# Two fp32 product stages in eight array tiles each, a third stage's four banks, and two products of the main stage in another place

## The reference, cut to what matters

```python
W = W_sess[session_ids]                        # [64 batches, 32, 64]
h = einsum('bct,bch->bht', x * cmask, W) + b   # 64 hidden values, per batch
h = gelu(h)                                    # erf form
out = einsum('bht,hs->bst', h, W2) + b2        # back to 32
c = out * tmask
x = x + (c.astype(fp16) @ W16 + bias)          # W16: int4 weights unpacked, 512 x 512
```

## Time and profile before

| | |
|---|---|
| median of 3 runs | 200.32 us (200.03 to 200.41) |
| the profiled execution | 200.16 us, of it a span of 198.4 us from first to last instruction |
| granted TensorE clock | 1.0 of full speed over the span |
| TensorE busy | 187.1 us (94%) |
| VectorE busy | 131.1 us (66%) |
| ScalarE busy | 69.2 us (35%) |
| GpSimd busy | 62.9 us (32%) |

### The profile page before, as it was taken

The page is one execution under the profiler, slowest core; times in us unless marked ns, Lnnn a source line. Parts: engine busy times, 40 slices in busy tenths (PEclk is TensorE's granted clock), DMA queues, the critical chain, the costliest instruction groups (busy, mean ns, idle before and its releaser), DMA issues.

```text
span 198.4 us, 3202 instructions
## 1 busy us (share of the span) xinstructions
PE 187.1 (94%) x962; PEld 124.1 (63%) x962; DVE 131.1 (66%) x319; ACT 69.2 (35%) x134; POOL 62.9 (32%) x91
## 2 busy tenths in 40 slices
PE   2889999789999999999999999999999999999993
PEld 1778656456675556565656566565667678688882
DVE  3697995477733677878785867577662689522961
ACT  0557636224314435552545344543522300031000
POOL 5273200000552266425652453321347223111000
PEclk9999999999999999999999999999999999999999
DMA  4899506069696252225112521151244943633993
GB/s 142 272 309 217 183 4 208 0 194 327 150 386 232 73 160 76 60 60 163 53 55 60 165 63 53 53 159 43 80 134 137 348 153 113 198 114 106 362 344 143
DMA packets 25785, 30.50 MB, mean 154 GB/s; under 512 B 7464, under 2 KB 16808, under 8 KB 25768
## 3 DMA queue, kind: packets, MB, share of 16 engines
q1 hardware_dynamic: 21968, 20.25, 32.5%
q0 software_dynamic: 3328, 9.96, 16.2%
q10 hardware_dynamic: 472, 0.09, 0.2%
HBM read 19.54 MB, written 6.55 MB: 132 GB/s over the span
## 4 chain that ended last, share of the span: by engine, by line
PE 90%; DVE 3%; DMA 2%; issue 2%; ACT 1%; SPq 0%; DVEq 0%
PE ps L1103 19%; PE ps L1015 9%; PE ps L1051 8%; PE ps L1027 8%; PE ps L988 6%; PE ps L962 6%; PE ps L1078 4%; PE ps L1061 4%; PE ps L1107 3%; PE ps L1076 3%; PE ps_ct L1103 3%; PE ps L1090 3%; PE ps L1003 2%; DMA x_all<-in_L_ffn_W 2%; PE ps_ct L1039 2%
## 5 line engine op out<-in xcount | busy, mean ns | idle before, releaser
L1103 PE MATMUL ps<-G,xT_all 128*128 128x512 f32 x168 | 48.9, 414 | 0.0
L341 POOL DMA_INDIRECT lz<-L_z_dram,idx_l x16 | 16.1, 1009 | 80.5 <-PE ps L1090 52.0
L1103 PEld LDWEIGHTS ps<-G,xT_all 128*128 128x128 f32 x168 | 29.0, 189 | 15.2 <-issue 11.0
L392 ACT ACTIVATE xT_all<-ps 128x512 fp32r<-128x512 f32 (+1 forms) x36 | 14.8, 453 | 43.8 <-PE ps L1061 33.9
L548 DVE TENSOR_TENSOR xT_all<-ps,xT_all 128x512 fp32r<-128x512 f32 (+2 forms) x37 | 18.9, 512 | 16.2 <-ACT xT_all L392 15.7
L448 ACT ACTIVATE gel<-ps,bsess 128x512 f32<-128x512 f32 x32 | 20.3, 684 | 17.2 <-PE ps L1015 17.2
L350 POOL DMA_INDIRECT WT<-L_dram,idx_l x16 | 15.3, 958 | 21.3 <-PE ps L1107 16.5
L324 POOL DMA_INDIRECT wsel<-in_L_cond_W_sess,idx_w x16 | 17.3, 1084 | 7.2 <-DVE onehot L552 4.2
L548 DVE TENSOR_TENSOR x_all<-x_all,ps 128x512 f32<-128x512 f32 x21 | 13.5, 682 | 8.8 <-PE ps L1239 8.6
L1015 PE MATMUL ps<-x_all,wbd 64*128 64x512 f32 x64 | 18.1, 641 | 0.0
L1051 PE MATMUL ps<-W,cT 128*128 128x512 f16 x64 | 16.6, 382 | 1.3 <-issue 1.2
(11 more groups left out here) (188 smaller groups left out, 274.5 us busy)
## 6 DMA issues: line engine op xcount, KB each, us to landing
az<-AT SPq DMA_DIRECT2D x64, 64.0 KB, 1.8
out<-x_all SPq DMA_DIRECT2D x15, 256.0 KB, 2.8
x_all<-in_x SPq DMA_DIRECT2D x3, 1024.0 KB, 6.4
L_dram<-xT_all SPq DMA_DIRECT2D x4, 512.0 KB, 8.9
x_all<-in_L_ffn_W SPq DMA_DIRECT2D x2, 512.0 KB, 4.3
x_all<-in_L_cond_base_weight SPq DMA_DIRECT2D x4, 256.0 KB, 7.4
x_all<-in_x SPq DMA_DIRECT2D x2, 512.0 KB, 5.9
x_all<-in_L_cond_lora_B_w SPq DMA_DIRECT2D x4, 256.0 KB, 8.0
```

What stands on the lines that cost most here:

```text
L341: nc.gpsimd.indirect_dma_start(lz[:, t % 2, :].bitcast(F32), None, L_z_dram, bass.IndirectOffsetOnAxis(idx_l[:, t:t + 1], 0)).then_inc(s_l ...
L392: return nc.scalar.activation(dst, src, ACT.Copy)
L1103: mm(dst, xT_all[:, t, a * KC + j, :], G[:, c, j, :], start=i == 0, stop=False, skip_group_check=True)
```

## The change

The eight blocks of `hidden` (four batches, two halves of 256 steps) and of `cond` become eight products each, on eight separate parts of the array, with weights without zero blocks (`wch` of 32 x 64, `W2h` of 64 x 32). From tile 3 on `hidden` writes its four batches to four banks, one of them `ffn`'s and one `cond`'s; tiles 0 to 2 use two banks and do their batches in two halves (`s_hid2`). ScalarE's `gelu` becomes four instructions of 256 columns, and VectorE's `make_c` two. New waits keep the shared banks apart: `hidden` waits for `make_c` and, from tile 3, for `f_copy`; `ffn` waits for the first `gelu` instruction. In the loop two products of `main` stand between `h_to_z` and `ffn`, and none between `h_transpose` and `c_transposes`. A few set-up instructions fall away (`m2`, the clearing of `W2bd`).

```diff
-        ps_hid, ps_c, ps_f, ps_x, ps_z = ps[0:2], ps[2], ps[4], ps[5], ps[6]
+        ps_f, ps_x, ps_z = ps[4], ps[5], ps[6]
+        HD = D // 2
+        gel_q = gel[:, :, :].rearrange("p a (b n) -> p (a b) n", b=2)
+        c_half = [ps[2][:, 0:HD], ps[0][:, HD:D]]
+
+        def hid_out(t, q):
+            if t < 3:
+                return ps[q % 2][:, HD * (q // 2):HD * (q // 2) + HD]
+            return ps[(0, 1, 2, 4)[q]][:, 0:HD]
...
                 nc.gpsimd.tensor_tensor(
-                    wbd[:, t % 2, :, :], wsel[:, t % NW, :].unsqueeze(1).to_broadcast([P, 2, HID]),
-                    mch[:, t, :].unsqueeze(2).to_broadcast([P, 2, HID]), ALU.mult).then_inc(s_wbd, 1)
+                    wch[:, t % 2, :], wsel[:, t % NW, :], mch[:, t:t + 1].to_broadcast([P, HID]), ALU.mult).then_inc(s_wbd, 1)
...
-                for p in range(2):
-                    nc.scalar.activation(gel[:, p, :], ps_hid[p][:, :], ACT.Gelu,
-                                         bias=bsess[:, 2 * t + p:2 * t + p + 1]).then_inc(s_gelu, 1)
+                for q in ((0, 1, 2, 3) if t < 3 else (3, 2, 0, 1)):
+                    nc.scalar.activation(gel_q[:, q, :], hid_out(t, q), ACT.Gelu,
+                                         bias=bsess[:, BT * t + q:BT * t + q + 1]).then_inc(s_gelu, 1)
...
-                stt(c16[:, :], ps_c[:, :], b2col[:, :], mask16[:, :], ALU.add, ALU.mult).then_inc(s_c16, 1)
+                for u in range(2):
+                    part = slice(HD * u, HD * u + HD)
+                    last = stt(c16[:, part], c_half[u], b2col[:, :], mask16[:, part], ALU.add, ALU.mult)
+                last.then_inc(s_c16, 1)
...
-            def hidden(t):
+            def hidden(t, batches):
+
                 pe.wait_ge(s_wbd, t + 1)
                 pe.wait_ge(dma[in_group(t)], 16)
                 if t == 0:
                     pe.wait_ge(s_bs, 1)
                 else:
-                    pe.wait_ge(s_gelu, 2 * t)
-                for p in range(2):
-                    half = slice(P // 2 * p, P // 2 * (p + 1))
-                    last = mm(ps_hid[p][:, :], wbd[half, t % 2, :, :].rearrange("p a h -> p (a h)"), x_all[half, t, :],
-                              start=True, stop=True)
-                last.then_inc(s_hid, 1)
+                    pe.wait_ge(s_gelu, BT * t)
+                    pe.wait_ge(s_c16, t)
+                if t >= 3:
+                    pe.wait_ge(s_f16, t - 1)
+                elif batches[0] > 0:
+
+                    pe.wait_ge(s_hid2, t + 1)
+                for u in range(2):
+                    for q in batches:
+                        rows = slice(C * q, C * q + C)
+                        last = mm(hid_out(t, q)[HID * u:HID * u + HID, :], wch[rows, t % 2, :],
+                                  x_all[rows, t, HD * u:HD * u + HD], start=True, stop=True)
+                last.then_inc(s_hid if BT - 1 in batches else s_hid2, 1)
 
             def cond(t):
-                pe.wait_ge(s_gelu, 2 * t + 2)
+
+                pe.wait_ge(s_gelu, BT * t + BT)
                 if t == 0:
                     pe.wait_ge(dma["w2"], 16 * 3)
                     pe.wait_ge(s_Rz, 1)
-                else:
-                    pe.wait_ge(s_c16, t)
-                for p in range(2):
-                    last = mm(ps_c[2 * C * p:2 * C * p + 2 * C, :], W2bd[:, :, :].rearrange("p a s -> p (a s)"),
-                              gel[:, p, :], start=True, stop=True)
+                for q in range(BT):
+                    for u in range(2):
+                        half = slice(HID * u, HID * u + HID)
+                        last = mm(c_half[u][C * q:C * q + C, :], W2h[half, :], gel_q[half, q, :], start=True, stop=True)
                 last.then_inc(s_cond, 1)
...
+                if 2 <= t < NT - 1:
+                    pe.wait_ge(s_gelu, BT * (t + 1) + 1)
...
-            hidden(0)
-            G_products(3)
+            hidden(0, (0, 1))
+            G_products(3, (0,))
+            hidden(0, (2, 3))
+            G_products(3, (1, 2, 3))
...
             for n in range(3, NT):
-                t, at = n // 3 - 1, 5 * (n % 3)
-                hidden(n)
+                t, i = n // 3 - 1, n % 3
+                hidden(n, range(BT))
                 h_to_z(n - 3)
+                if i > 0:
+                    main(t, 5 * i - 2, 2)
+                elif t > 0:
+                    main(t - 1, NP, 2)
                 ffn(n - 1)
                 h_and_z(n - 2)
                 cond(n)
-                if n % 3 == 0 and t > 0:
+                if i == 0 and t > 0:
                     pe.wait_ge(s_evac, t)
-                main(t, at, 3 if n % 3 < 2 else 2)
+                main(t, 5 * i, 3 if i < 2 else 2)
                 x1_transposes(n - 1)
                 h_transpose(n - 2)
-                main(t, at + (3 if n % 3 < 2 else 2), 2)
                 c_transposes(n)
 
 
-            main(4, 5, 4)
+            main(4, 3, 6)
```

More of the change, by code:

```diff
@@ L67, in adaln_ffn_program @@
         wsel = sb("wsel", [P, NW, HID], F32)
-        wbd = sb("wbd", [P, 2, 2, HID], F32)
+        wch = sb("wch", [P, 2, HID], F32)
         lz = sb("lz", [P, 2, 2 * ZW], F32R)
@@ L82, in adaln_ffn_program @@
         m4 = sb("m4", [P, 4, BT], F32)
-        m2 = sb("m2", [P, 2], F32)
         hmask = sb("hmask", [P, BT, RK], F32)
@@ L90, in adaln_ffn_program @@
         q_shift = sb("q_shift", [P, 1], I32)
-        mch = sb("mch", [P, NT, 2], F32)
-        bsess = sb("bsess", [P, NT * 2], F32)
-        W2bd = sb("W2bd", [P, 2, C], F32)
+        mch = sb("mch", [P, NT], F32)
+        bsess = sb("bsess", [P, NB], F32)
+        W2h = sb("W2h", [P, C], F32)
         b2col = sb("b2col", [P, 1], F32)
@@ L569, in _ @@
             link(nc.vector.tensor_copy(oddp[:, :], pid_f[:, 3:4]))
-            link(tt(m2[:, :], m32[:, 0:2], m32[:, 2:4], ALU.add))
             link(nc.vector.tensor_copy(m4[:, :, :], m32[:, :].unsqueeze(1).to_broadcast([P, 4, BT])))
@@ L620, in _ @@
             dve.wait_ge(s_bsp, 1)
-            nc.vector.tensor_copy(bsess[:, :], ps[1][:, 0:2 * NT]).then_inc(s_bs, 1)
+            nc.vector.tensor_copy(bsess[:, :], ps[1][:, 0:NB]).then_inc(s_bs, 1)
             dve.wait_ge(dma["q"], 16)
@@ L697, in constant_rows_of_Bstk @@
                     dve.wait_ge(s_crow, 1)
-                    dve.wait_ge(s_masks, 4)
+                    dve.wait_ge(s_masks, 3)
                     link(nc.vector.tensor_copy(f32r_row[last, :], crow[last, :]))
@@ L765, in add_main @@
                 tt(x_all[:, t, :], x_all[:, t, :], main_bank[t][:, :], ALU.add).then_inc(s_evac, 1)
-            dve.wait_ge(s_masks, 3)
+            dve.wait_ge(s_masks, 2)
             time_mask(0)
@@ L865, in _ @@
             dve.wait_ge(dma["lrow"], 16)
-            dve.wait_ge(s_masks, 5)
+            dve.wait_ge(s_masks, 4)
             link(tt(BD.rearrange("p (t r) -> p t r", t=NT), blk[:, :, 0:1].to_broadcast([P, NT, R32]),
@@ L947, in b_session, with G_products @@
                 pe.wait_ge(dma["bsess_in"], 16)
-                oh = onehot[:, :].rearrange("s (n a) -> s a n", a=2)
-                for a in range(2):
-                    last = mm(ps[1][HID * a:HID * a + HID, 0:2 * NT], b_raw[:, :], oh[:, a, :], start=True, stop=True)
+                for u in range(2):
+                    last = mm(ps[1][HID * u:HID * u + HID, 0:NB], b_raw[:, :], onehot[:, :], start=True, stop=True)
                 last.then_inc(s_bsp, 1)
-            def G_products(j):
+            def G_products(j, ks=range(KC)):
                 pe.wait_ge(s_WTlo, j + 1)
@@ L957, in G_products @@
                     pe.wait_ge(s_ids, 2)
-                for k in range(KC):
+                for k in ks:
                     if j == 0 and k == 2:
@@ L1123, in _ @@
             A_transposes(0, (s_Glo, 2))
+            hidden(1, (0, 1))
             A_transposes(1, (s_Glo, 3))
-            hidden(1)
+            hidden(1, (2, 3))
             pe.wait_ge(s_lBlo, KC)
@@ L1135, in _ @@
             L(1, (s_Alo, 4))
+            c_transposes(1)
+            hidden(2, (0, 1))
             x1_transposes(0)
-            c_transposes(1)
-            hidden(2)
+            hidden(2, (2, 3))
             L(2, (s_Lz, 1))
@@ L1176, in _ @@
             h_transpose(NT - 2)
-            pe.wait_ge(s_gelu, 2 * NT)
+            pe.wait_ge(s_c16, NT)
             main(5, 0, 7)
@@ L1183, in _ @@
             h_transpose(NT - 1)
-            pe.wait_ge(s_gelu, 2 * NT)
+            pe.wait_ge(s_gelu, BT * NT)
             main(6, 0, 5)
```

11 lines of the change are left out of this document (3 added, 8 removed).

## The result

The changed kernel takes 201.09 us (median of 6 runs, 200.60 to 201.58), the kernel before 200.18 beside it: a ratio of 1.0046 (95% interval 1.0025 to 1.0067), slower by 0.9 us.

The account below looks back on a forecast made before the run. The prediction took the ring, a closed path through several engines, to bound the loop. 200.16 + 0.3 (prologue) + 1.1 (loop) - 0.25 (tail) = 201.3, 201.5 in medians; it said 201.4 us, range 200.3 to 203.4.

Parts of the forecast that it names:

- The eight tiles: In `cond` and `hidden`: all eight run side by side, 0.60 us per stage, 0.41 less for `cond`, 0.46 for `hidden`.
- the rival of four or two tiles at a time: In `cond` and `hidden`, not all tiles run at once: about 204.5 us (chance 0.08) or over 220 (0.01).
- E: The moment in a loop pass when the row of the last `h_and_z` product ends on TensorE.
- The ring: Loop path from E through `make_x1`, `x1_transposes`, `hT_lo`, `h_to_z`, TensorE to next E: 6.51 us against 6.42.
- sign of being wrong: In the loop: passes under 6.4 us, or `h_to_z` starting right behind `hidden`.
- The rival in which the ring is not closed: In the loop, `h_to_z` gets its data before TensorE comes: pass 6.06, about 196 us; chance 0.12.
- The loop's term: Twelve loop passes, each 0.09 us longer: +1.1 us (0.4 to 2.4).
- rival "no change": In the loop, GpSimd's halved product disturbs `make_x1` less, 0.68 each: ring 6.45, 200.3 to 200.5 us; chance 0.16.
- The prologue: Tiles 0 to 2, before the loop: halved `hidden` costs more, `cond` gives some back; sum +0.3 us (-0.1 to 0.7).
- The set-up: Before the first tile: the removed steps lie under the wait for the first weights, so nothing was charged.
- The tail: After the loop: `ffn(15)` comes about 0.25 us earlier, then the same round, and the rest shifts as a whole.
- Emptying PSUM: Rival on ScalarE's copies: a `gelu` staying at 0.68 pushes `sum_hz` back some 0.15 per pass, 203.3 us; chance 0.05.

## Why the prediction was right, and where it was wrong

**The eight tiles** were costed right: `cond` takes 0.59 us where I said 0.60, and `hidden` 0.61 in the run where the products of `main` stand right behind it (97.70 to 98.31). Against the 1.01 of two tiles of 512 columns that is 0.42 for two passes of 256 columns, 0.21 each as I had it. That rules out the rival of four or two tiles at a time, whose own sum was wrong: `cond` at 1.01 brings TensorE to E - 0.06 + 1.01 + 0.69 = E + 1.64, 0.29 over E + 1.35 with three products of `main` and 0.06 with two, some 0.2 on average and not 0.15. A `gelu` of 256 columns takes 476 ns (I said 473), half of `make_c` 475 (480), four `gelu` together 1.57 us (1.58).

**The ring** was right. The three waits stand where I put them, by the moments of the pass above: `x1_transposes` at E + 1.29 (I said 1.35), `c_transposes` E + 2.28 (2.35), `hidden` E + 2.62 (2.70), `h_to_z` E + 3.68 (3.75), the next E at 6.44 (6.51); all passes are alike, where before two of three took 6.50 and the third 6.27. TensorE's busy time fell by 8.1 us, where I had said some 10. One reading was too wide: the earlier trace rows shows `x1_transposes` starting the moment its data is there in a pass with two products of `main`; in the two passes with three its load came 0.22 and 0.11 behind the end of `make_x1` (103.93, 110.43), so there TensorE was the late one before. That the moved products are on it is shown three ways: put back, put one place up, and moved alone. Neither sign of being wrong came up: the passes are not under 6.4, and 0.37 lie between `hidden` and `h_to_z`. The rival in which the ring is not closed gave 196 us, with a pass of 6.06; with the products off the ring the pass is 6.13 and the time 196.7 to 197.2.

**The loop's term was mis-sized.** I said +1.1 us, and the loop costs 0.15. Of the difference 0.84 are twelve passes each 0.07 shorter than I said, and 0.10 comes from counting: the loop before takes 77.12 by `cond` and 77.02 by `hidden`. The 0.07 lies in the first step, up to `x1_transposes`: I took 0.74 us for `make_x1` as in one row, and it now takes 0.68 in every pass (679 to 683 ns). Over the loop of the kernel before it averages 0.76. The 0.03 for the change of data type ahead of `ffn` has no row of its own in any run; with `ffn` it made 0.91, and 6.44 less the rest of the ring (5.90 - 0.13 - 0.23) leaves 0.90.

My rival "no change" had the 0.68, and its ring of 6.45 is the measured one. Its reason was GpSimd's halved product, and that is not needed for it. Before, the product does lengthen `make_x1` in four passes:

```profile
110.00 0.58 POOL L333 TENSOR_TENSOR wbd<-wsel,mch 128x128 f32<-128x128 f32 x1
```

It runs from 110.00, into the second half of the `make_x1` that starts at 109.47 and takes 0.85. In the pass that I took the 0.74 from there is no product beside it; a gather of GpSimd starts 0.02 behind it. After, the two of the pass at the same place:

```profile
109.53 0.68 DVE L553 TENSOR_TENSOR x_all<-x_all,f 128x512 f32<-128x512 f32 x1
...
109.64 0.72 POOL L340 TENSOR_TENSOR wch<-wsel,mch 128x64 f32<-128x64 f32 x1
```

Now GpSimd's product starts 0.11 behind `make_x1` and is itself the one that is stretched, to 0.72 where another pass of it takes 0.30. Not only the size of the product changed, its start moved too. The run with the move alone tells the two apart, for there the product has its old size:

```profile
111.98 0.68 DVE L548 TENSOR_TENSOR x_all<-x_all,f 128x512 f32<-128x512 f32 x1
...
112.08 0.84 POOL L333 TENSOR_TENSOR wbd<-wsel,mch 128x128 f32<-128x128 f32 x1
```

It starts 0.10 to 0.21 behind `make_x1`, and `make_x1` takes 0.68 in all four passes. With the halved product and the products put back it starts 0.44 to 0.54 behind, and `make_x1` takes 0.68 to 0.78. So the start decides, and the size only how much: some 0.55 behind, the old product made it 0.89 and the halved one 0.78 to 0.79. The move alone is enough for the 0.68; without it the halved product helps, to 0.70 on average over the loop.

**The prologue** was right, in its steps too: counted from `hidden(0)`, `ffn(0)` comes 0.19 later (I said 0.2), the gain of `cond(1)` goes into the wait for `AT` (1.01 in place of 0.59), and `L(3)` loses 0.28 behind `x1_transposes(1)` (I said some 0.2). In all +0.33 up to `hidden(3)` and +0.40 up to `cond(3)`, against +0.3. The same 43.9 us stand between `hidden(0)` and `cond(3)` in all but one of the ten profiles with these tiles (44.2 with the repeated emptying, which begins at tile 3), and 43.5 in the four with the old products.

**The set-up** I had at nothing, and in the profiled pair it is -0.37. `hidden(0)` starts at 20.09 on the mean of nine profiles with the new set-up and at 20.51 on that of three with the old, but the ranges (19.92 to 20.43, 20.32 to 20.69) overlap, and the times can't confirm a gain.

**The tail was wrong in its second half.** Up to `h_and_z(15)` it gains 0.50, where I said 0.25: 0.39 up to `ffn(15)`, and 0.11 in the round behind it, where `make_x1` takes 0.68 in place of 0.81. Then I wrote "from there the round of the earlier trace rows is the same, and the rest shifts as a whole". It does not: TensorE's lead meets the gather of tile 5, which is issued later than before, and 0.75 us are lost. I had followed each wait of the loop to what is late next, and not the last lead of the tail. The early gather takes the loss away (41.73).

So the mechanism of the loop was right, and the number was in part luck. The forecast of 201.4 came out near 201.09 because errors cancel: a loop 0.95 too dear and a set-up whose -0.37 I did not have, against a tail 0.50 and a prologue 0.10 too cheap. They leave 0.72 too much for the profiled execution (200.60), which is the fastest of its six; the median lies 0.5 above it, and no trace shows where. That the kernel is slower, and not the same, comes from the prologue (+0.40) and the tail (+0.25) more than from the loop (+0.15), which the ring leaves as long as it was.

**Emptying PSUM** is not the limit here: with one more `gelu`, or one more half of `make_c`, a pass grows by 0.00 and 0.02. The Trainium skill's page "TensorEngine Tiling (Array Packing)", section "PSUM Bottleneck", warns that after a fourfold speed-up of TensorE the emptying may become the bottleneck. Here `cond` became 1.7 times as fast (1.01 to 0.59), and the warning comes true only in the run with both repeats in front of bank 4's `gelu`: 0.40 more on that round cost 0.02 a pass, 0.77 more 0.31, and the 0.44 that lies to spare is worked out from the trace, not measured by a run.

## What to carry to other kernels

When TensorE is at 90% of the chain, look for a place in the trace where it has less to do, and read there how long the other engines' round is: that length, and not TensorE's saving, is what a faster TensorE stage gets. In a program written in order, work that is moved costs nothing in front of a wait; behind it, it costs up to its length, as far as no other wait takes its place (here 0.31 of 0.55 us a pass); one place up or down was 3.7 us here. And follow a lead to its end: here a transfer that another engine issues at its own time took it back.

## What was not expected of the hardware

VectorE and GpSimd can lengthen one another's steps when they overlap, and in these traces which of the two pays changes with their offset. In the loop it was `make_x1` (0.85 in place of 0.68) when GpSimd's product came 0.53 behind its start, and the product (0.72 in place of 0.30) when it came 0.11 behind. Wherever the product starts while `make_x1` runs, it ends a fixed time behind it: 0.25 us with the old size (16 pairs in four traces), 0.15 with the halved one (36 pairs in nine).

In the tail a masking step of GpSimd took 0.40 before, where it began 0.06 ahead of a `make_x1` that took 0.81 (a clearing of GpSimd began 0.49 behind it, so which of the two lengthened it is not told apart), and 0.83 after, where it began 0.11 behind one that took 0.68. The lead itself brought them together: this `make_x1` starts 0.21 earlier than before, the masking step 0.04. The longer step delayed the gather, and that is part of the wait of 1.25 us. The other traces agree, with one exception: in all seven where the gather stands behind a masking step of 0.78 to 0.83 the wait is 1.12 to 1.26, in three of the four where that step takes 0.40 it is 0.37 to 0.39, and in the fourth (the move alone) 0.78, with a transfer that took 0.4 longer to land.
